# Delta's parts stored in five copies instead of eight, the scan's first matrix loaded in sixteen pieces, two casts moved to ScalarE

## The reference

```python
delta = softplus(dt_r @ W_dt + b_dt)
A = -jnp.exp(A_log)

def step(h, inputs):
    d_t, B_t, C_t, u_t = inputs
    dA = jnp.exp(d_t[:, :, None] * A)
    h = h * dA + (d_t * u_t)[:, :, None] * B_t[:, None, :]
    y_t = jnp.einsum('bdn,bn->bd', h, C_t)
    return (h, y_t)
```

## Time and profile before

| | us |
|---|---|
| median of 3 runs | 5962.3 (5960.25 to 5962.47) |
| profiled execution | 5963.24 |
| its span | 5961.4 |
| VectorE busy | 5410.5 (91%) |
| TensorE busy | 5294.7 (89%) |
| ScalarE busy | 3425.7 (57%) |
| GpSimd busy | 2280.8 (38%) |

### The profile page before, as it was taken

How to read it: one execution, slowest core, us unless ns; L and a number is a source line. 1 busy time by engine, 2 the same in 40 slices (tenths; PEclk the granted TensorE clock), 3 DMA queues, 4 the chain that set the end, 5 groups by cost and what they waited for, 6 DMA issues and landing times. The chain is left out here.

```text
span 5961.4 us, 148751 instructions
## 1 busy us (share of the span) xinstructions
PE 5294.7 (89%) x38396; PEld 2512.2 (42%) x38396; DVE 5410.5 (91%) x3476; ACT 3425.7 (57%) x8110; POOL 2280.8 (38%) x6767
## 2 busy tenths in 40 slices
PE   2999959999999999999999999999999999979999
PEld 1444424444444444444444444444444444436665
DVE  5799989999999999999999999999999999963433
ACT  6777746666666666666666666666666666631111
POOL 4000024444444444444444444444444444420000
PEclk6999879999999999999999999999999999989999
DMA  4899952222222222222222222222222222233322
GB/s 159 299 334 334 339 170 54 55 52 54 54 55 52 54 55 53 53 54 55 51 54 55 54 52 54 55 52 54 55 55 51 54 55 53 53 101 109 105 96 67
DMA packets 1105508, 547.16 MB, mean 92 GB/s; under 512 B 753744, under 2 KB 1015056, under 8 KB 1105056
## 3 DMA queue, kind: packets, MB, share of 16 engines
q1 hardware_dynamic: 1093776, 533.89, 33.7%
q10 hardware_dynamic: 11664, 12.52, 0.6%
HBM read 296.83 MB, written 249.82 MB: 92 GB/s over the span
## 5 line engine op out<-in xcount | busy, mean ns | idle before, releaser
L988 DVE TENSOR_TENSOR_SCAN s_h<-s_decay,s_ubank 128x1024 f32<-128x1024 f32 x2048 | 4460.7, 2262 | 11.7 <-ACT s_ubank L953 10.4
L940 ACT ACTIVATE s_decay<-s_abank 128x512 f32<-128x512 f32 x4096 | 2207.9, 595 | 2.1 <-PE s_abank L878 1.1
L863 PE MATMUL s_ybank<-s_h,s_window 128*8 128x256 f32 x16416 | 1948.2, 602 | 1.9 <-DVE s_h L988 1.9
L904 PE MATMUL s_ubank<-s_x,s_w 128*128 128x256 bf16 x8192 | 1245.6, 275 | 374.2 <-DVE s_h L988 373.8
L1024 POOL TENSOR_TENSOR s_carry<-s_decay,s_h 128x64 f32<-128x64 f32 x2032 | 880.6, 433 | 1752.4 <-ACT s_decay L940 1576.3
L953 ACT ACTIVATE s_ubank<-s_seed 128x64 f32<-128x64 f32 x2048 | 479.9, 234 | 1712.2 <-PE s_ubank L904 1314.1
L878 PE MATMUL s_abank<-xnT,s_a 128*128 128x256 bf16 x8192 | 1254.9, 274 | 32.8 <-DMA s_w<-scratch_b_rows 29.9
L904 PEld LDWEIGHTS s_ubank<-s_x,s_w 128*128 128x128 bf16 x8192 | 675.5, 98 | 1196.4 <-DVE s_h L988 1096.9
L878 PEld LDWEIGHTS s_abank<-xnT,s_a 128*128 128x128 bf16 x8192 | 758.3, 98 | 195.5 <-ACT s_decay L940 36.9
L863 PEld LDWEIGHTS s_ybank<-s_h,s_window 128*8 128x8 f32 x16416 | 378.0, 97 | 838.5 <-issue 729.5
L1028 POOL TENSOR_TENSOR s_seed<-s_carry,s_first 128x64 f32<-128x64 f32 x2048 | 656.8, 321 | 164.1 <-ACT s_first L946 3.6
(11 more groups left out here) (123 smaller groups left out, 2965.6 us busy)
## 6 DMA issues: line engine op xcount, KB each, us to landing
s_x<-scratch_u_rows SPq DMA_DIRECT2D x4096, 32.0 KB
scratch_u_rows<-p_u_turn SPq DMA_DIRECT2D x90, 1024.0 KB, 6.6
scratch_delta_rows<-p_dparts SPq DMA_DIRECT2D x136, 512.0 KB, 6.2
xnT<-scratch_delta_rows SPq DMA_DIRECT2D x1024, 64.0 KB, 2.8
scratch_y<-s_y SPq DMA_DIRECT2D x1036, 16.0 KB
scratch_sz<-p_sz SPq DMA_DIRECT2D x16, 1024.0 KB, 6.2
scratch_u<-p_u SPq DMA_DIRECT2D x16, 1024.0 KB, 7.9
s_w<-scratch_b_rows SPq DMA_DIRECT2D x256, 64.0 KB, 2.4
```

The lines of the kernel that those rows point to most:

```text
L863: last = nc.tensor.matmul(y_bank[32 * ct:32 * ct + WIN, 1 - x, :], window[:, of, (at + t) * WIN:(at + t + 1) * WIN], H[:, 1 - x, :, t], st ...
L904: last = nc.tensor.matmul(dst.rearrange("p q (a t) -> p a q t", t=2), w2[:, g, 4 * s + 2 * x + e, :], x2[:, s, :, 2 * x + e, q:q + 32, :], ...
L940: nc.scalar.activation(dst.rearrange("p x q t -> p q x t"), a_bank[:, b].rearrange("p j r (x t) -> p (j r) x t", x=2), ACT.Exp).then_inc(e ...
L988: nc.vector.tensor_tensor_scan(H[:, x, PT * p:PT * p + PT, :].rearrange("p q t -> p (q t)"), decay[:, x * (1 + c % 2), p].rearrange("p q t ...
```

## The change

`delta_rows` becomes `[PLACES, DI, TOK + TW]`, and `back_stores` stores five copies instead of eight, behind a wait for delta's second part too. In the scan a row's 16 partitions (eight copies x two halves) come from five copies in two overlapping loads: copies 0 to 3 into 8 partitions and 1 to 4 into the next 8, which gives the parts 0,1,2,0 and 1,2,0,1 as before. The bytes of these loads stay the same, their number doubles. In the projections the second casts of delta and du, which VectorE did at L691, become `second_delta` and `second_u` on ScalarE, between v and the exponential; VectorE's `split` now does the first cast and the rest of delta, the first cast and the rest of du, then waits for ScalarE's second part of delta; the last part of du comes after the split of B (`split_last`). Two memsets start `w1` and `du` at zero, and the semaphores are counted to match.

```diff
             def back_stores(i, c, b):
+                sp.wait_ge(d2_done, i + 1)
                 sp.wait_ge(d3_done, i + 1)
-                for k, (_, j) in reversed(list(enumerate(COMBOS))):
+                for k, (_, j) in reversed(list(enumerate(COMBOS[:PLACES]))):
                     sp.dma_start(tile_of(d["delta_rows"][k], i), dparts[:, j]).then_inc(dparts_stored, 16)
...
+            def second_delta(i):
+                act.wait_ge(dr_done, i + 1)
+                nc.scalar.activation(dparts[:, 1], w1[:, :, :], ACT.Identity).then_inc(d2_done, 1)
+
+            def second_u(i):
+                act.wait_ge(ur_done, i + 1)
+                nc.scalar.activation(uparts[:, 1], du[:, :, :], ACT.Identity).then_inc(u2_done, 1)
...
+                second_delta(i)
                 act.wait_ge(back_read, i * 7 + 12)
                 nc.scalar.activation(ex[:, :, :], v[:, :, :], ACT.Abs).then_inc(abs_done, 1)
+                second_u(i)
                 act.wait_ge(abs_done, i + 1)
                 nc.scalar.activation(ex[:, :, :], ex[:, :, :], ACT.Exp, scale=-1.0).then_inc(exp_done, 1)
...
             def split(i):
...
+                dve.wait_ge(delta_done, i + 2)
+                dve.wait_ge(dparts_stored, i * (16 * PLACES) + 16 * PLACES)
+                nc.vector.tensor_copy(dparts[:, 0], lw[:, :, :]).then_inc(d1_done, 1)
+                dve.wait_ge(d1_done, i + 1)
+                nc.vector.tensor_tensor(w1[:, :, :], lw[:, :, :], dparts[:, 0], ALU.subtract).then_inc(dr_done, 1)
+                dve.wait_ge(du_done, i + 3)
+                dve.wait_ge(turned, i * 8 + 16)
+                nc.vector.tensor_copy(uparts[:, 0], du[:, :, :]).then_inc(u1_done, 1)
+                dve.wait_ge(u1_done, i + 1)
+                nc.vector.tensor_tensor(du[:, :, :], du[:, :, :], uparts[:, 0], ALU.subtract).then_inc(ur_done, 1)
+                dve.wait_ge(d2_done, i + 2)
+                nc.vector.tensor_tensor(dparts[:, 2], w1[:, :, :], dparts[:, 1], ALU.subtract).then_inc(d3_done, 1)
...
+            def split_last(i):
+                dve.wait_ge(u2_done, i + 3)
+                nc.vector.tensor_tensor(uparts[:, 2], du[:, :, :], uparts[:, 1], ALU.subtract).then_inc(u3_done, 1)
...
                     for r in range(ROWS):
-                        src = deltas[r, :, :, :, bass.ds(f * T + TW, 2 * T)]
-                        sp.dma_start(x1[16 * r:16 * r + 16, g, r], src).then_inc(rows_loaded[g], 16)
+                        for lo in range(2):
+                            at = 16 * r + 8 * lo
+                            src = deltas[r, 2 * lo:2 * lo + 8, :, :, bass.ds(f * T + TW, 2 * T)]
+                            sp.dma_start(x1[at:at + 8, g, r], src).then_inc(rows_loaded[g], 16)
...
-    scratch("delta_rows", [NCB, DI, TOK + TW], BF16)
+    scratch("delta_rows", [PLACES, DI, TOK + TW], BF16)
```

More of the change, by code:

```diff
@@ L481, in _ @@
             sp.wait_ge(sz_stored, 16 * (NT + 1))
-            sp.wait_ge(dparts_stored, 16 * NCB * (NT + 1))
+            sp.wait_ge(dparts_stored, 16 * PLACES * (NT + 1))
             sp.wait_ge(c_stored, 16 * (NT + 1))
@@ L518, in turn @@
                 if g == 0:
+                    pe.wait_ge(u2_done, i + 1)
                     pe.wait_ge(u3_done, i + 1)
@@ L557, in _ @@
             act.sem_inc(turn_read, 11)
+            act.sem_inc(u2_done, 1)
             act.wait_ge(weights, 16 * n_weights)
@@ L622, in take_turn @@
                                              ACT.Identity).then_inc(turn_read, 1)
+            act.wait_ge(cleared, 4)
             for m in range(8):
@@ L630, in _ @@
                     take_turn(i, g)
+                if i == NT:
+                    second_delta(NT)
+                    second_u(NT)
         @block.vector
@@ L634, in _ @@
             dve.sem_inc(delta_done, 1)
+            nc.vector.memset(w1[:, :, :], 0.0).then_inc(dr_done, 1)
+            nc.vector.memset(du[:, :, :], 0.0).then_inc(ur_done, 1)
             nc.vector.memset(uparts[:, :, :, :], 0.0).then_inc(cleared, 1)
@@ L713, in step @@
                 split_b(i)
+                split_last(i)
             front(0, 0, 0)
@@ L872, in logits @@
                 if kk == 0 and s == 0:
-                    pe.wait_ge(rows_loaded[g], it * 176 + 176)
+                    pe.wait_ge(rows_loaded[g], it * 304 + 304)
                 for b in range(2):
@@ L1003, in lay_window @@
                 s, g = c % 2, c // 2
-                pool.wait_ge(rows_loaded[g], it * 176 + 176)
+                pool.wait_ge(rows_loaded[g], it * 304 + 304)
                 pool.wait_ge(y_ready, f * 2 + 1)
```

## The result

The changed kernel takes **7155.4 us** (median; 7152.0 to 7157.6) where the kernel before took 5961.4 beside it: a ratio of 1.200, 95% interval 1.198 to 1.202. It is 1194 us slower. The forecast was 6279, with a range from 5970 to 6500. The sign was right and the size was far off.

What follows compares the result with a forecast made beforehand. VectorE's chain of recurrences was taken to bound the scan. 5963.2 + 4 (tiles) - 4.5 (end of projections) + 3.5 (loads at scan start) + 314 (scan stalls) = 6280, or 6279 against the median; range 5970 to 6500.

Steps and rivals of the forecast that it cites:

- What bounds the kernel: In the scan, VectorE's chain of 2048 recurrences, 2.18 us apart; anything that holds one up is paid in full.
- Price of an issue: Scan: each new load costs SyncE 0.41 us, 0.59 with the gap; sixteen make it 3.5 us later every two chunks.
- rival 4: Scan: each new load costs 0.564 us, SyncE 5.9 late, stall 4.9: 6588 us and more; chance 0.09.
- The cover: Scan: of SyncE's 3.5 us, 0.63 hidden at the B loads, 0.2 at the u loads' landing, 0.2 at VectorE.
- the 0.2: Scan: the last u load lands 0 to 0.6 us ahead of the matmul needing it; 0.2 us taken as hidden.
- The clock: Scan: TensorE's clock falls to 0.50 behind the stall, 1.0 us more a period, 127 us: 6406; chance 0.20.
- the forecast's own stall of 2.47: Scan: SyncE's lateness less what is hidden, 2.47 us every two chunks (0.3 to 4.9), 314 us over 127 periods.
- costs nothing: Projections: SyncE's new wait for delta's second part comes earlier than its existing wait for the third, so adds no time.
- The projections: Per tile +0.3 us (-0.4 to +0.5) with the casts on ScalarE; over 13 tiles +4 us (-5 to +7).
- the ring: Projections, an engine's time per tile: VectorE 34.1 us, TensorE 36.2, ScalarE with the casts 36.5 to 37.1.
- rival 5: Projections: ScalarE's waits for TensorE shrink, VectorE's 34.1 us sets the tile, scan loads are hidden: 5930 us; chance 0.07.
- The tail: End of the projections: three fewer stores in each of three tiles bring -4.5 us (0 to -8).

Runs made afterwards that it cites:

- the padded change: The whole change with 120 instructions put on SyncE ahead of the scan loop: 6962.2 us, 1.168 against the kernel before.
- two rows split: The kernel before with two of its eight rows each loaded by two loads of 8 partitions, from eight copies: 6395.5 us (1.073).
- the casts alone: The change with the eight copies and eight loads of before, leaving only the casts on ScalarE: 6146.8 us, 1.031 against the kernel before.
- the kernel with two queues: The whole change with each row's upper-half load issued on ScalarE's queue, the lower on SyncE's: 6036.3 us, 1.012 against the kernel before.

## Why the prediction was wrong

- *What bounds the kernel.* Right. VectorE bounds the scan, and SyncE's lateness is paid in full. The chain that I read, from SyncE's loads over the firsts and the seed to VectorE, is the one in which the stall stands.
- *Price of an issue.* **The step that failed most.** I took 0.41 us on a straight line between 0.278 and 0.564, and the bounds from those two rows. It is 0.676, outside both, so that even rival 4 (*dear issues*, 6588 and more, chance 0.09) was priced too low. The line assumed that the cost rises with the rows of the transfer, or with the partitions; but the load with half of the partitions and half of the rows is dearer than the whole one. What the sequencer does there no trace shows. With 0.863 from one to the next sixteen are 7.81 us later instead of 3.5, and 127 x 7.81 = 992 instead of 314. The trace of before could have warned: the load of C, 128 rows of 256 bytes, costs 0.478 against 0.278 for u's 32 rows, at the same bytes. I named that row and kept the bound.
- *The cover.* Read too large at one place. The firsts begin 1.75 us after the last issue of u ends in the padded change (3119.69 to 3121.44), where TensorE waits for that load, and 1.73 in the kernel before (3040.85 to 3042.58), where the profile shows no wait. So there was nothing hidden at the landing, and the 0.2 was wrong. The 0.63 ahead of the B loads was real: that wait is gone. What a period at full clock hides is 0.75 us (two rows split), where I had read 1.03.
- *The clock.* I made it a rival at 0.20. It is there in every period and costs what I gave it, 1.0 us. It should have been a term of the sum: its condition (TensorE without work as long as in the earlier trace rows, 1.92 us) followed from the forecast's own stall of 2.47.
- *The refetch.* Not in the sum nor in any rival: 178 us with the casts alone, 193 in the change. The view was open, the line of instruction packets with 44, and nobody can forecast from it that 327 lies five behind 322. That SyncE's new wait "costs nothing" was wrong in this sense: where the casts stand alone, it is this wait's nine instructions ahead of the loop that bring the whole 178 us, as eight idle ones bring 177 to the kernel before. And that the change puts 48 instructions into a loop and takes others out ahead of it could have been a rival with a row.
- *The projections.* Forecast 36.9 us a tile; the one shown has 35.5, where before had 36.6. Over all tiles it is less, 35.9 from the first to the last (205.6 to 744.4) against 36.2 (202.2 to 744.9): the last splits end at 768.6 against 771.84, 3.2 us earlier, where I had summed to 3.2 later. The rows are of line 685 (the 1.0 added, the former line 666) in two tiles, ScalarE's logarithm, TensorE's third projection, and two waits:

```profile
389.97 1.23 DVE L685 TENSOR_SCALAR p_w<-p_ex 128x2048 f32<-128x2048 f32 x1
425.45 1.23 DVE L685 TENSOR_SCALAR p_w<-p_ex 128x2048 f32<-128x2048 f32 x1
...
391.25 1.91 ACT L612 ACTIVATE p_lw<-p_w 128x2048 f32<-128x2048 f32 x1
...
430.15 1.13 PE L495 MATMUL p_in<-xnT,p_w_in 128*128 x2 [0.94 <-ACT p_xi L570]
...
ACT p_v L603 <- PE p_bk L512: 29.7, 47, 1.3
...
DVE p_dparts L711 <- ACT p_dparts L577: 26.8, 12, 4.7
```

  ScalarE's wait ahead of the logarithm is gone, and VectorE waits 2.2 us a tile for ScalarE's part of Delta, where I had 2.1: the ring has closed over ScalarE as forecast. The tile is shorter than I summed. I had counted ScalarE's waits for TensorE as fixed. The one for v did stay (28.6 us in 47 before, 29.7 in 47 after), but the one ahead of the emptying of the projections' banks (L567, now L570) fell from 14.1 us to 8.0 in these 12 tiles: 0.5 us a tile gave way, as rival 5 said, only by less.
- *The tail.* The scan's stage begins 6.9 us earlier (791.54 against 798.46); with 3.2 of them from the tiles the tail gives 3.7, forecast 4.5. The sixteen loads take that back: the first recurrence comes 0.5 us later than before, where the forecast's terms came to 3.0.

So the sum would have been right with 7.81 for 3.5, no net cover (some 0.8 us hidden and some 1.0 lost to the clock), and the refetch, with both of the last two taken from the runs: 5963 + 0 + 992 + 193 = 7148, where the profiled span and what lies around it came to 7152.

## What to carry to other kernels

Count a queue's issues by the exact form of the transfer, and where that form is not in the trace, bound it above as well as below by something outside the two nearest rows: halving a load doubled the issues and made each dearer. Where a queue is late, look for a wait in its own order first; moving half of the loads ahead of a wait of 7 us brought back 832 of 1000 us with the same number of loads. And when a kernel changes by a few per cent in a stage whose code is untouched, look at the row of the instruction queue: SyncE's loop, once it touched a fourth block of 128 instructions, was fetched again in every pass, and idle instructions ahead of it mended that. (That fewer instructions inside would do the same follows from the theory; no run tried it.)

## What was unexpected of the hardware

- A loop of 322 instructions with its third block boundary at 327 ran without refetch, and at 325 with it. The boundaries are 128 instructions apart. With the refetch, SyncE's gap at the branch was 3.0 to 3.9 us instead of 0.7, and the kernel lost 177 to 222 us over 64 passes.
- A load of 8 partitions with 256 rows of 128 bytes takes the issuing engine 0.676 us on SyncE and 0.687 on ScalarE; with 16 partitions and 512 such rows 0.564; with 8 partitions and 32 rows of 1 KB 0.278.
- In the padded change TensorE's clock was 0.50 from 3121 to 3127, behind a wait of 4.5 us, and 1.00 again from 3130; with VectorE's stalls of 0.4 to 0.7 us (the kernel with two queues) it stayed at 1.00 over the scan, and so it did at the stall of 1.0 us with two rows split.
